# First attention layer: masks and half of the weight splits change engines

## The reference

```python
h = relu(layernorm(x))                                  # 4096 x 256
s = h @ W @ a[:256];  r = h @ W @ a[256:]
e = leaky_relu(s + r.T, 0.2)                            # 4096 x 4096
p = softmax(where(adj > 0,  e, -1e12), axis=1)
q = -softmax(where(adj > 0, -e, -1e12), axis=1)
x = x + elu(concat([p @ h, q @ h], axis=1) @ wtrans)    # first layer
h = relu(layernorm(x))
for W_l in W_stack:                                     # two more layers
    Wh, Ws = split(h @ W_l)
    h = leaky_relu((softmax(Wh @ Ws.T) * adj) @ Wh + h, 0.01)
x = x + h
```

## Time and profile before

| | |
|---|---|
| median of 3 runs | 2611.19 us (2610.53 to 2612.25) |
| the profiled execution's own time | 2612.48 us |
| its span, first to last instruction | 2610.7 us |
| phase `l0b`, from the first mask to the last x1 | about 66 to 929 us |
| mean granted TensorE clock | 0.983 of full speed |
| busy shares of the span | PE 95%, PEld 90%, DVE 85%, ACT 65%, POOL 58% |

### The profile page before, as it was taken

How to read it: one execution, slowest core, us unless ns; L and a number is a source line. 1 busy time by engine, 2 the same in 40 slices (tenths; PEclk the granted TensorE clock), 3 DMA queues, 4 the chain that set the end, 5 groups by cost and what they waited for, 6 DMA issues and landing times. The chain is left out here.

```text
span 2610.7 us, 47736 instructions
## 1 busy us (share of the span) xinstructions
PE 2480.9 (95%) x18360; PEld 2346.5 (90%) x18360; DVE 2210.9 (85%) x2942; ACT 1694.8 (65%) x2348; POOL 1523.2 (58%) x932
## 2 busy tenths in 40 slices
PE   4699999999999979999999999987999999999997
PEld 2588888888888869999999999987999999999997
DVE  8899999998989646888888888894788888888888
ACT  6899999999999754555555555553555555555554
POOL 3899999999999802444434444350245445444446
PEclk8799999999999989999999999999999999999999
DMA  3332323233323021333333333233133333333333
GB/s 109 107 94 89 94 90 93 91 95 93 95 90 93 13 100 47 96 97 107 94 98 102 98 96 107 90 114 109 58 101 114 102 95 120 95 105 111 102 98 106
DMA packets 100980, 248.21 MB, mean 95 GB/s; under 512 B 9360, under 2 KB 51088, under 8 KB 100752
## 3 DMA queue, kind: packets, MB, share of 16 engines
q1 hardware_dynamic: 98880, 243.30, 30.5%
q10 hardware_dynamic: 1872, 1.84, 0.2%
HBM read 232.52 MB, written 12.58 MB: 94 GB/s over the span
## 5 line engine op out<-in xcount | busy, mean ns | idle before, releaser
L91 PE MATMUL l0b_acc<-l_h_parts,l0b_turned_hi 128*128 128x512 f32 x1984 | 727.2, 406 | 19.3 <-POOL l0b_turned_lo L541 19.2
L541 POOL TENSOR_TENSOR l0b_turned_lo<-l0b_turned,l0b_turned_hi 128x1024 fp32r<-128x1024 f32 x256 | 614.3, 2416 | 45.0 <-ACT l0b_turned_hi L578 43.3
L92 PE MATMUL l0b_acc<-l_h_parts,l0b_turned_lo 128*128 128x256 f32 x1984 | 558.3, 281 | 0.0
L1133 POOL TENSOR_TENSOR g0b_sum_wide<-g0b_sum_wide,g0b_slab 128x512 f32<-128x512 f32 x240 | 311.3, 1297 | 396.1 <-DVE g0b_masked_psum L1241 386.0
L1133 POOL TENSOR_TENSOR g1b_sum_wide<-g1b_sum_wide,g1b_slab 128x512 f32<-128x512 f32 x240 | 315.5, 1315 | 339.5 <-DVE g1b_masked_psum L1241 328.7
L91 PEld LDWEIGHTS l0b_acc<-l_h_parts,l0b_turned_hi 128*128 128x128 f32 x1984 | 376.0, 190 | 112.7 <-POOL l0b_turned_lo L541 29.7
L92 PEld LDWEIGHTS l0b_acc<-l_h_parts,l0b_turned_lo 128*128 128x128 f32 x1984 | 374.2, 189 | 0.8
L578 ACT CAST l0b_turned_hi<-l0b_turned 128x1024 fp32r<-128x1024 f32 x256 | 268.1, 1047 | 67.6 <-PE l0b_acc L92 50.1
L80 PE MATMUL g0b_acc<-g_wh_parts,g0b_part_hi 128*128 128x256 f32 x1024 | 293.6, 287 | 6.8 <-DVE g0b_part_lo L1247 5.7
L80 PE MATMUL g1b_acc<-g_wh_parts,g1b_part_hi 128*128 128x256 f32 x1024 | 293.6, 287 | 5.6 <-DVE g1b_part_lo L1247 4.5
L80 PE MATMUL g0b_score_psum<-g0b_q_block,g_vt_hi 128*128 128x256 f32 x1024 | 290.3, 284 | 2.5 <-DVE g0b_q_block L1277 1.4
(11 more groups left out here) (231 smaller groups left out, 7218.6 us busy)
## 6 DMA issues: line engine op xcount, KB each, us to landing
g_adj_ring<-in_adj_blocks_dram SPq DMA_DIRECT2D x256, 512.0 KB, 3.6
l_adj_ring<-in_adj_quads_dram SPq DMA_DIRECT2D x128, 512.0 KB, 3.5
l0b_x_in<-in_x_dram SPq DMA_DIRECT2D x32, 128.0 KB, 2.4
x_rows<-l0b_x SPq DMA_DIRECT2D x32, 128.0 KB, 2.4
g0a_rows<-x_rows SPq DMA_DIRECT2D x8, 512.0 KB, 5.8
g0b_y<-x_rows SPq DMA_DIRECT2D x16, 256.0 KB, 4.0
v_rows<-g0b_y SPq DMA_DIRECT2D x16, 256.0 KB, 4.5
g1a_rows<-v_rows SPq DMA_DIRECT2D x8, 512.0 KB, 5.8
```

The costliest lines, as they stand in the source:

```text
L91: pe.matmul(out, lhs_hi, rhs, start=first, stop=False)
L92: return pe.matmul(out[:, width:], lhs_lo, rhs[:, :width], start=False, stop=False)
L541: pool.tensor_tensor(turned_lo[:, m % PART_RING, :, :], turned[:, m % TURN_RING, :, :], turned_hi[:, m % PART_RING, :, :].bitcast(F32), AL ...
L1133: pool.tensor_tensor(sum_wide[:], sum_wide[:], half_of(c, e), ALU.add).then_inc(summed, 1)
```

## The change

ScalarE makes the mask of every piece, in `score(f)`, right ahead of the wait for `masked` and of the score. GpSimd's `penalty`, the tile `unit` and the semaphore `penalty_ready` go, and with them VectorE's wait for it. Of the splits, ScalarE keeps those of even groups (so it splits at even steps alone). For odd groups GpSimd waits for the turned weights and for a free slot, casts the high part itself, waits for its own cast, and subtracts.

```diff
-                    def penalty(f):
-                        slot = adj_ring[:, f % ADJ_SLOTS, :]
-                        pool.wait_ge(adj_in[f % ADJ_SLOTS], 16 * (f // ADJ_SLOTS + 1))
-                        pool.tensor_tensor(slot, slot, unit[:].to_broadcast([P, PIECE]), ALU.subtract
-                                           ).then_inc(penalty_ready, 1)
-
                     def rest(m):
-                        pool.wait_ge(hi_ready, m + 1)
                         wait(pool, products, m - PART_RING + 1)
+                        high = turned_hi[:, m % PART_RING, :, :]
+                        if m % 2 == 0:
+                            pool.wait_ge(hi_ready, m // 2 + 1)
+                        else:
+                            pool.wait_ge(turns, m + 1)
+                            pool.tensor_copy(high, turned[:, m % TURN_RING, :, :]).then_inc(odd_hi_ready, 1)
+                            pool.wait_ge(odd_hi_ready, m // 2 + 1)
                         pool.tensor_tensor(turned_lo[:, m % PART_RING, :, :], turned[:, m % TURN_RING, :, :],
-                                           turned_hi[:, m % PART_RING, :, :].bitcast(F32), ALU.subtract
-                                           ).then_inc(lo_ready, 1)
+                                           high.bitcast(F32), ALU.subtract).then_inc(lo_ready, 1)
...
-                    penalty(1)
-                    for n in range(STEPS):
-                        f, odd = divmod(n, 2)
-                        if odd == 0 and f + 2 < T * 4 and (f + 2) % 4 != 0:
-                            penalty(f + 2)
-                        if 0 <= n - TO_SPLIT < FRONTS:
-                            rest(n - TO_SPLIT)
+                    for m in range(FRONTS):
+                        rest(m)
...
                     def score(f):
                         t, a = divmod(f, 4)
-                        if a == 0:
-                            slot = adj_ring[:, f % ADJ_SLOTS, :]
-                            act.wait_ge(adj_in[f % ADJ_SLOTS], 16 * (f // ADJ_SLOTS + 1))
-                            act.activation(slot, slot, ACT.Copy, bias=-1.0)
+                        slot = adj_ring[:, f % ADJ_SLOTS, :]
+                        act.wait_ge(adj_in[f % ADJ_SLOTS], 16 * (f // ADJ_SLOTS + 1))
+                        act.activation(slot, slot, ACT.Copy, bias=-1.0)
                         wait(act, masked, 2 * (f - 1))
...
-                        if 0 <= n - TO_SPLIT < FRONTS:
+                        if 0 <= n - TO_SPLIT < FRONTS and (n - TO_SPLIT) % 2 == 0:
                             split(n - TO_SPLIT)
...
                         dve.wait_ge(score_ready, tau + 1)
-                        if a:
-                            dve.wait_ge(penalty_ready, 3 * t + a)
```

More of the change, by code:

```diff
@@ L178, in first_block @@
         fold = keep.sbuf("fold", [P, 4, QUAD])
-        unit = keep.sbuf("unit", [P, 1])
         wt_hi = keep.sbuf("wt_hi", [P, 2 * KT, D], F32R)
@@ L248, in _ @@
                     pool.memset(ones[:], 1.0).then_inc(ones_made, 1)
-                    pool.memset(unit[:], 1.0)
                     identity_matrix(pool, ident_plain, zeroed, ident_done)
@@ L455, in first_block @@
             padded = mem.sem("padded")
-            penalty_ready = mem.sem("penalty_ready")
+            odd_hi_ready = mem.sem("odd_hi_ready")
             score_ready = mem.sem("score_ready")
```

## The result

| | before | after |
|---|---|---|
| median | 2611.70 us (4 runs, 2610.53 to 2612.25) | 2707.75 us (4 runs, 2702.71 to 2726.34) |
| ratio | | 1.0382, 95% interval 1.0349 to 1.0415 |
| span of the profiled execution | 2610.7 us | 2700.6 us (its own time 2702.71) |
| mean granted clock | 0.983 | 0.966 |

The change makes the kernel 3.8% slower. The forecast of "no change" was wrong, and 2707.75 lies just above the range's end of 2705. The mechanism of rival 1 is what happened, in 22 of 29 tiles of the profiled execution, with more lost clock than the range took in. (That execution took 2702.71 us, the shortest of the four; the others have no trace in which tiles could be counted.)

What follows compares the result with a forecast made beforehand. The prediction took the longest closed path through a ring of engines as the bound, 25.90 us a tile. 2612.5 + 29 x (25.86 - 25.90) + 1.3 = 2612.6, adjusted to the median: 2612 us; range 2598 to 2705.

Steps and rivals of the forecast that it cites:

- no change: Whole kernel: 2612 us forecast, tiles of 25.86 us against 25.90; chance 0.43.
- rival 1: At L696 GpSimd is first and holds VectorE's addition: +2.3 us a tile, 2679 us, up to 2720 with lost clock; chance 0.25.
- The paths: Closed paths through the engines in l0b; the second, through ScalarE's splits and L696, sums to 25.86 us a tile.
- Is L696 free?: Step comparing starts after the split of step 2: addition at 14.24, GpSimd's subtraction at 14.29; VectorE first by 0.02 to 0.05.
- the term 13.15: Time in us from ScalarE's split of step 2 to its split of step 6, read near the stage's end.
- 1.14: Time in us from ScalarE's split of step 6 to GpSimd's start on group 0's subtraction, giving 14.29.
- the free side: At L696 VectorE is first and the addition takes 0.42 us: 2612 us; chance 0.43.
- the two that hold: GpSimd first at L696 in every tile, chance 0.25, or in a third to two thirds of tiles, chance 0.15.
- the full rival: GpSimd first at L696 in every tile: 2679 us, up to 2720 if half clock rate adds 1.5 us a tile; chance 0.25.
- Rival 2: At L696 both orders occur by turns, GpSimd first in a third to two thirds of tiles: 2634 to 2656 us; chance 0.15.
- the fill: While the pipeline fills, up to two more masks lie ahead of the first group: 0 to 1.9 us, taken as 1.3.
- no one waits for ScalarE in odd steps: ScalarE's load: the 4 casts removed lie in odd steps, claimed to hold up no one; load falls 0.95 us a tile.

Runs made afterwards that it cites:

- e1_swap6: Changed kernel with ScalarE's exponential ahead of the split in steps 6, so GpSimd's subtraction of group 0 starts about 0.9 us later; 2613.75 us.
- e4_psum: Changed kernel with the first of the last part's two additions written to PSUM, so the addition of x_in has one SBUF input; 2612.64 us.
- e2_delay: Changed kernel with one small reduction (128x2, about 0.16 us) on VectorE just ahead of the addition of x_in; 2615.03 us.
- e8_odd_psum: Changed kernel with one input of the x_in addition in PSUM and ScalarE's mask moved from the even step to the odd step before; 2581.29 us.
- e5_late: Changed kernel with four small reductions (128x2) on VectorE ahead of the addition of x_in; 2704.30 us.
- e11_splits: Kernel before with half the change: GpSimd makes both parts of every second group and keeps all masks; 2700.31 us.

## Why the prediction was wrong, point by point

**The paths were right.** Counted from the split of step 2, the changed kernel has L674 at 4.69 to 4.70 (forecast 4.70), the split of step 4 at 6.56 to 6.58, now released by VectorE's turn (forecast 6.54 to 6.57), the addition at 14.27 or 14.28 (forecast 14.24 to 14.27). Here are, of the tile whose addition starts at 433.83, the split of step 2, L674, the split of step 4 and L668:

```profile
419.55 1.05 ACT L569 CAST l0b_turned_hi<-l0b_turned 128x1024 fp32r<-128x1024 f32 x1 [3.19 <-PE l0b_acc L92]
...
424.25 0.69 DVE L674 TENSOR_TENSOR l0b_means_lo<-l0b_means_psum,l0b_means_hi 128x512 fp32r<-128x512 f32 x1 [3.47 <-ACT l0b_means_hi L581]
...
426.12 1.05 ACT L569 CAST l0b_turned_hi<-l0b_turned 128x1024 fp32r<-128x1024 f32 x1 [0.77 <-DVE l0b_turned L651]
...
430.70 0.48 DVE L668 SCALAR_TENSOR_TENSOR l0b_means<-l0b_acc,l0b_inverse,l0b_means 128x256 f32<-128x256 f32 x1 [1.21 <-ACT l0b_means L576]
```

Where nothing holds the addition, tiles are 25.9 us (forecast 25.86) and TensorE's wait at L719 is 0.73:

```profile
439.31 0.33 PE L719 MATMUL l0b_side_psum<-all_ident_r,l0b_max_parts 128*128 128x128 f32 x1 [0.73 <-DVE l0b_max_parts L626]
```

e1_swap6 and e4_psum are the kernel that the forecast of 2612 describes, and take 2613.75 and 2612.64.

**The step that failed is "Is L696 free?", by the term 13.15.** I took the split of step 6 at 13.15 behind that of step 2, from one tile near the stage's end, and GpSimd's start 1.14 behind it, at 14.29. Measured, the split of step 6 comes at 13.02 to 13.05 in the 22 held tiles and at 13.11 to 13.13 in the 7 free ones, and GpSimd starts 1.19 to 1.20 behind it, at 14.22 to 14.25 or at 14.30 to 14.33. The addition, at 14.27 or 14.28, stands between the two. So two terms were off: 13.15 was 0.11 too long for a held tile, and 1.14 was 0.06 too short, which gave half of it back. With the addition at the late end of my 14.24 to 14.27, the lead of 0.02 to 0.05 that I gave VectorE became one of 0.03 to 0.05 for GpSimd. The value 13.15 does occur, in 27 tiles of e2_delay (13.15 to 13.18), and one row could not tell which of the values comes. The same 0.1 us would not have mattered at any other place of the sum.

**The chances** leaned on that lead. The two estimated starts lay closer together than the rows they came from scatter, so both orders should have weighed alike; I gave the free side 0.43, and the two that hold 0.40 together. e2_delay, which turned 22 held tiles into 2 with one 0.16 us instruction, shows how little such a side can be known beforehand.

**The clock was named for the full rival only, and left out of the mixed one.** Rival 2 (by turns) was priced at 2634 to 2656 with 2.3 us a held tile. Each held tile cost 1.8 more by the clock, a little over the 1.5 that I had as a bound. With 4.1 us a held tile, the two thirds of rival 2 would have given 2691, and the 22 of 29 that were held 2702.

**What held:** GpSimd's cast takes 1.04 (forecast 1.04); VectorE's dropped wait and adj's DMA cost nothing; the masks in even steps were costed rightly at 0.95 each, and e8_odd_psum shows that they ate the gain. **What also failed, at little cost:** the fill, 2.8 us instead of 1.3. The 0.42 of a free addition came out right, but the row that it was taken from (L326) is a multiplication of the same size, not an addition. And the sentence that no one waits for ScalarE in odd steps doesn't fit and the earlier trace rows, where GpSimd waits 1.01 us for the split of group 7; the sum is untouched, since GpSimd's own cast takes as long.

**Open:** why TensorE comes to the end of step 5 at one of two times, 0.09 us apart, and why nearly the same gap takes the clock in each of 22 tiles of the changed kernel (1.8 us a tile on average) and in every second one of e5_late (0.8). Neither was tried.

## What to carry to other kernels

Where several engines are near their limit, add up the closed paths, not the loads: relief on GpSimd was worth 30 us here (17 with the addition's second SBUF input left in) as soon as what it was bought with lay in steps that no one waits behind, and nothing while it lay ahead of a score. Look for every VectorE instruction with two SBUF inputs beside GpSimd work: its price here wasn't its own 0.42 us but up to 2.25 of GpSimd's 2.42, and an input moved to PSUM took the risk away. And where a forecast rests on who is first by less than the rows scatter, it has no likeliest side; take the tie away in the code instead of guessing it.

## What the runs showed of the hardware

- VectorE's 0.42 us addition with two SBUF inputs was held for 2.25 us when GpSimd's subtraction started 0.03 to 0.05 us ahead, and delayed GpSimd by 0.25 when it was itself ahead; with one input in PSUM it was held in none of 29 tiles. A cast of GpSimd (1.04) held it in the same way, in all 29 tiles of e11_splits.
- The granted clock fell behind all 22 gaps of 3.04 to 3.17 us on TensorE in the changed kernel (in the tile shown, 0.52 for some 3.5 us) and behind 15 of 29 gaps of 3.04 to 3.16 us in e5_late, every second one. Behind 20 small matmuls and 0.86 to 0.88 us of idleness it fell in 2 of 13 tiles; with 26 small matmuls and 0.19 to 0.31 us of idleness in none of 29.
- At a granted clock of 1.00, TensorE's pairs of L91 and L92 came at two paces in the same kernel. Below are two matmuls of L91, eight pairs apart, 10 us behind the split of step 2 in the held tile (split at 389.83), and the same of the free tile (split at 419.55). The eight pairs take 2.77 us in the one, 0.346 each, and 2.83 in the other, 0.354 each. So 0.06 us arises in this stretch alone, which is of the size of the tie. The pace doesn't decide alone, though: the held tile whose split of step 2 is at 272.74 has the slower one (285.88 - 283.05 = 2.83 us for eight pairs) and an earlier start. What sets the pace was not tried.

```profile
399.85 0.39 PE L91 MATMUL l0b_acc<-l_h_parts,l0b_turned_hi 128*128 128x512 f32 x1
...
402.62 0.39 PE L91 MATMUL l0b_acc<-l_h_parts,l0b_turned_hi 128*128 128x512 f32 x1
...
429.60 0.39 PE L91 MATMUL l0b_acc<-l_h_parts,l0b_turned_hi 128*128 128x512 f32 x1
...
432.43 0.39 PE L91 MATMUL l0b_acc<-l_h_parts,l0b_turned_hi 128*128 128x512 f32 x1
```
